# A conditional mix with a mixture of low-rank experts: one engine's bias held back, splits and tails reordered in the first three steps, half of a product moved in the last

## The reference, cut to what matters

```python
x, cond                      # x: (64, 64, 1024) f32, cond: (64,) in 0..15
y = einsum('bct,bcd->bdt', x, W[cond])          # 64 x 64 per batch, 16 conditions
logits = einsum('bsd,ed->bse', y, gate_w)       # 8 experts, the best 2 chosen
gates  = softmax of the best 2, zero elsewhere
low    = einsum('bsd,erd->ebsr', y, lora_A)     # rank 16 for each of 8 experts
result = y @ base_w.T + base_b + 2 * einsum('ebsr,eor,bse->bso', low, lora_B, gates)
out = x + result
```

## Time and profile before

| | |
|---|---|
| time, median of 3 runs | 489.36 us (488.27 to 489.56) |
| time of the profiled execution | 488.3 us |
| its span, first to last instruction | 486.5 us |
| mean granted clock of TensorE | 0.993 |
| busy: PE, DVE, ACT, POOL | 473.6, 353.5, 159.9, 120.7 us |
| moved by DMA | 76.91 MB, mean 158 GB/s |

### The profile page before, as it was taken

How to read it: one execution, slowest core, us unless ns; L and a number is a source line. 1 busy time by engine, 2 the same in 40 slices (tenths; PEclk the granted TensorE clock), 3 DMA queues, 4 the chain that set the end, 5 groups by cost and what they waited for, 6 DMA issues and landing times.

```text
span 486.5 us, 8142 instructions
## 1 busy us (share of the span) xinstructions
PE 473.6 (97%) x2660; PEld 464.0 (95%) x2660; DVE 353.5 (73%) x636; ACT 159.9 (33%) x262; POOL 120.7 (25%) x113
## 2 busy tenths in 40 slices
PE   8995999999999999999999999999999999999996
PEld 8995998989999999999999999999999999999995
DVE  4858679778686785868678685876868677585843
ACT  5723533233332233323323332233324223332300
POOL 2346033132041402304141140413104141310300
PEclk9998999999999999999999999999999999999999
DMA  8972353534626264362536436253552526343202
GB/s 319 412 243 90 148 186 116 177 108 165 204 88 220 63 222 146 141 223 88 187 93 215 152 129 215 84 197 108 190 177 113 208 84 224 109 172 111 88 22 86
DMA packets 49275, 76.91 MB, mean 158 GB/s; under 512 B 13666, under 2 KB 32226, under 8 KB 49250
## 3 DMA queue, kind: packets, MB, share of 16 engines
q1 hardware_dynamic: 37586, 71.88, 42.1%
q10 hardware_dynamic: 11664, 4.72, 3.7%
HBM read 41.98 MB, written 34.60 MB: 157 GB/s over the span
## 4 chain that ended last, share of the span: by engine, by line
PE 89%; DVE 4%; ACT 3%; issue 2%; DMA 2%; ACTq 0%; POOL 0%; DVEq 0%; POOLq 0%
PE acc L886 44%; PE acc L878 27%; PE acc L924 9%; PE mixed L918 8%; DMA low_turns<-scratch 1%; PE acc L1082 1%; DVE y_lo L640 1%; DVE t_lo L604 1%; DVE x_parts L620 1%; ACT r_hi L445 1%; DMA scratch<-low_turns 1%; ACT y_hi L457 0%; DVE t_raw L611 0%; ACT y_whole L478 0%; ACT x_parts L467 0%
## 5 line engine op out<-in xcount | busy, mean ns | idle before, releaser
L382 POOL TENSOR_TENSOR x_sb<-x_sb,bias 128x1024 f32<-128x1024 f32 x32 | 77.3, 2438 | 217.6 <-DVE x_sb L732 198.0
L878 PE MATMUL acc<-r_hi,y_hi 128*128 128x392 f32 x256 | 88.3, 345 | 5.3 <-DVE x_sb L739 5.3
L878 PE MATMUL acc<-r_hi,y_lo 128*128 128x392 f32 x256 | 87.9, 344 | 0.2 <-DVE y_lo L599 0.2
L878 PE MATMUL acc<-r_lo,y_hi 128*128 128x392 f32 x256 | 87.7, 343 | 0.0
L886 PE MATMUL acc<-t_hi,s_hi 128*128 128x384 f32 x224 | 74.9, 334 | 1.0 <-issue 1.0
L886 PE MATMUL acc<-t_lo,s_hi 128*128 128x384 f32 x224 | 74.9, 334 | 0.0
L886 PE MATMUL acc<-t_hi,s_lo 128*128 128x384 f32 x224 | 74.8, 334 | 0.0
L886 PE MATMUL acc<-t_hi,y_hi 128*128 128x384 f32 x216 | 72.3, 335 | 0.0
L886 PE MATMUL acc<-t_lo,y_hi 128*128 128x384 f32 x216 | 72.3, 335 | 0.0
L886 PE MATMUL acc<-t_hi,y_lo 128*128 128x384 f32 x216 | 72.2, 334 | 0.0
L640 DVE TENSOR_TENSOR y_lo<-y_turned,y_hi 128x512 fp32r<-128x512 f32 x60 | 51.4, 896 | 26.9 <-ACT y_hi L513 26.8
(11 more groups left out here) (81 smaller groups left out, 740.7 us busy)
## 6 DMA issues: line engine op xcount, KB each, us to landing
x_sb<-in_x SPq DMA_DIRECT2D x32, 512.0 KB, 4.3
out<-x_sb SPq DMA_DIRECT2D x31, 512.0 KB, 3.1
y_scratch<-y_whole SPq DMA_DIRECT2D x60, 256.0 KB, 2.1
y_moved<-y_scratch SPq DMA_DIRECT2D x120, 128.0 KB, 2.8
t_raw<-in_w_quads SPq DMA_DIRECT2D x4, 768.0 KB, 9.4
scratch<-low_turns ACTq DMA_DIRECT2D x16, 128.0 KB, 1.8
low_turns<-scratch ACTq DMA_DIRECT2D x64, 32.0 KB, 2.3
r_raw<-in_w_plain SPq DMA_DIRECT2D x8, 196.0 KB, 5.2
```

The costliest lines, as they stand in the source:

```text
L382: nc.gpsimd.tensor_tensor(x_sb[:, slot(c), :], x_sb[:, slot(c), :], bias[:, :], ALU.add) \
L878: return nc.tensor.matmul(acc[:, i, 0:NP], y_part[:, i, k, :], w_part[:, k, :], start=(k == 0 and product == 0), stop=(k == KT - 1 and pro ...
```

## The change

- SyncE, step 0: of the two loads of x (c = 4 and 5) the second is issued after the move of pair 1, no longer ahead of it.
- GpSimd, steps 0 and 1: `add_bias` for the next step's pairs waits for `y_ready` 8 (both pairs of y split in step 0) and for `y_ready` 10 (pair 0 of y split in step 1).
- ScalarE, step 0: `lowT_high` goes behind `y_copy(0, 0, 1)` and the two `y_high` of pair 0; the cast of T1 goes behind those of pair 1.
- VectorE, step 0: `y_low` of pair 0 ahead of `lowT_low`; `finish_tails` ahead of the split of x; the first `t_add` last.
- VectorE, step 1: `t_low(2, T3)` comes in here (from step 2), `t_low(4, T4)` goes out (to step 2, behind the splits of the sums, `s_low`); `lowT_low` ahead of the split of x.
- Last step: VectorE does `lowT_low` ahead of the third `take`; TensorE does the first half of P4 (6 matmuls) ahead of its experts, the other 6 at the end as before.
- TensorE's waits on `t_ready` follow the new order of the splits. No instruction that computes or moves data is added or taken away.

```diff
@@ SyncE, step @@
                 if load:
-                    for i in range(2):
+                    for i in range(2 if u > 0 else 1):
...
                 if ahead:
                     move(j, u, 1)
+                if u == 0:
+                    load_x(j, 5)
@@ GpSimd, step @@
                     pool.wait_ge(bias_added, 2)
                     select(0, 0, 2)
+                    pool.wait_ge(y_ready, 8)
...
                     if u > 1:
                         pool.wait_ge(taken, 4 * (s - 2) + 3)
+                    else:
+                        pool.wait_ge(y_ready, 10)
@@ ScalarE, step 0 @@
-            lowT_high(0, 0)
             y_copy(0, 0, 1)
-            x_high(0, 0, 2)
             y_high(0, 0, 0, 0)
             y_high(0, 0, 0, 1)
-            t_high(1, T1)
+            lowT_high(0, 0)
+            x_high(0, 0, 2)
             y_high(0, 0, 1, 0)
             y_high(0, 0, 1, 1)
+            t_high(1, T1)
@@ VectorE, step 0 @@
             turn(0, 0, 0)
-            lowT_low(0, 0)
             y_low(0, 0, 0, 0)
             y_low(0, 0, 0, 1)
+            lowT_low(0, 0)
+            finish_tails(0, 0)
             x_low(0, 0, 2)
-            t_add(1, T1, raw_12, raw_11)
-            finish_tails(0, 0)
...
+            t_add(1, T1, raw_12, raw_11)
@@ VectorE, sums_step (step 1) @@
                 t_add(3, T2, raw_22, t_raw[:, T1, :, :])
+                t_low(2, T3)
                 x_low(j, u, 1)
...
+                lowT_low(j, u)
                 x_low(j, u, 2)
-                t_low(4, T4)
-                lowT_low(j, u)
@@ VectorE, step (2 to 15) @@
+                if u == 2:
+                    t_low(4, T4)
                 if ahead:
                     x_low(j, u, 1)
...
-                if u == 2:
-                    t_low(2, T3)
...
-                take(j, u, 2, 5, 1, 0, 2 * BW)
-                lowT_low(j, u)
+                if ahead:
+                    take(j, u, 2, 5, 1, 0, 2 * BW)
+                    lowT_low(j, u)
+                else:
+                    lowT_low(j, u)
+                    take(j, u, 2, 5, 1, 0, 2 * BW)
@@ TensorE, last_products @@
                 multiply(C22, summed(S3), factor(T3), first=False).then_inc(prod_done, 1)
+                multiply(C21, half(1, 1), factor(T4), ks=range(HALF_K // 2))
                 pe.wait_ge(lowT_ready, s + 1)
                 plain_experts()
...
-                experts(1, C21, 0, BW, fresh=True)
+                experts(1, C21, 0, BW)
...
-                multiply(C21, half(1, 1), factor(T4), first=False).then_inc(lora_done, 1)
+                multiply(C21, half(1, 1), factor(T4), first=False, ks=range(HALF_K // 2, HALF_K)).then_inc(lora_done, 1)
```

More of the change, by code:

```diff
@@ L879, in plain, with multiply @@
                                         start=(k == 0 and product == 0), stop=(k == KT - 1 and product == last))
-            def multiply(bank, left, right, first=True):
+            def multiply(bank, left, right, first=True, ks=range(HALF_K)):
                 left_hi, left_lo = left
                 right_hi, right_lo = right
-                for k in range(HALF_K):
+                for k in ks:
                     for n, (l, r) in enumerate(((left_hi, right_hi), (left_hi, right_lo), (left_lo, right_hi))):
@@ L920, in mix, with experts @@
                     last.then_inc(mix_done, 1)
-            def experts(i, bank, lo, hi, fresh=False):
+            def experts(i, bank, lo, hi):
                 for n, (low_part, lb_part) in enumerate(((lowT_hi, lb_hi), (lowT_hi, lb_lo), (lowT_lo, lb_hi))):
                     last = nc.tensor.matmul(acc[:, bank, 0:hi - lo], low_part[:, i, :], lb_part[:, lo:hi],
-                                            start=(fresh and n == 0), stop=(n == 2), skip_group_check=True)
+                                            start=False, stop=(n == 2), skip_group_check=True)
                 return last
@@ L1029, in step @@
                 if u == 2:
-                    pe.wait_ge(t_ready, 1)
+                    pe.wait_ge(t_ready, 2)
                 multiply(C22, summed(S2), factor(T2), first=False).then_inc(prod_done, 1)
@@ L1035, in step @@
                 if u == 2:
-                    pe.wait_ge(t_ready, 2)
+                    pe.wait_ge(t_ready, 3)
                 multiply(C21, half(1, 1), factor(T4)).then_inc(prod_done, 1)
@@ L1039, in step @@
                 pe.wait_ge(taken, 4 * (s - 2) + 2)
-                if u == 2:
-                    pe.wait_ge(t_ready, 3)
                 multiply(C22, summed(S3), factor(T3), first=False).then_inc(prod_done, 1)
```

## The result

The changed kernel takes **485.97 us** (median of 6, 485.46 to 487.02); the kernel before, timed beside it, 488.56 us. The ratio is 0.9949, with an interval from 0.9937 to 0.9960: faster by 0.5%, or 2.6 us. The forecast was 1.2 us faster, put as 488.1 us: it was taken from the first median of the kernel before, 489.36 us of three executions, and that of all six is 0.8 us lower. The profiled execution has a span of 483.9 us, 2.6 less than before. All executions of the kernel before that were timed beside the experiments have a median of 488.8 us.

A forecast was written before the change was run, and what follows sets the result against it. TensorE, busy for 97% of the span, was taken as the bound, so only its waits, slow clock and program ends could give time; +0.6 - 1.05 - 0.7 = -1.2 us, from 489.36 to 488.1 us; eight in ten from 485.2 to 489.8.

The forecast's parts named there:

- faster rival: Steps 0 and 1: either GpSimd takes fewer turns (486.4 us, chance 0.15) or `t_add` meets no contention (481.7 us, 0.07).
- the slower rival: Step 0: the second move lands late and delays pair 1's turn; over 490.8 us from 2.7 us late on, chance 0.13.
- its second rival: Step 1: no contention with the `t_add`, chain 4.7 us shorter, clock stays up; -7.65 us, 481.7 us, chance 0.07.
- the first case: Stall moves from step 0 to step 1's experts; around 488.1 us, own range 486.9 to 489.4, chance 0.65.
- the rival with fewer turns: Step 1: GpSimd's second addition slips behind the third `t_add`, what follows comes 1.8 us earlier; -3.0, 486.4 us, chance 0.15.
- start of step 2: End of step 1: experts resume 1.3 us earlier but the lower clock costs 1.9 us, so 0.6 us later.
- step 2: With `t_low(2, T3)` out of VectorE's queue, the second `take` precedes TensorE's arrival: -1.05 us; `t_low(4, T4)` stays hidden.
- last step, to the end of the span: Last matmul ends 1.4 us earlier, but the end is a store; -0.7 us taken, between -0.35 and -1.4.
- the two limits: Step 1: `lowT_lo` done at 76.7 us behind GpSimd's second addition, or 75.6 with the DMAs alone setting it.
- the stores' bound (0.35): Last step: the two stores before the last follow the last S1T1 product, which moves by 0.35 us only.
- TensorE's (1.4): Last step: six P4 matmuls fill the stall before the experts but for 0.35 us; last matmul ends 1.4 us earlier.

## Why the prediction was right, and what it mis-sized

**Right.** The stall moved, as forecast, from the tails of step 0 to the experts of step 1, for 6.2 us where 6.6 were said; the clock fell there and not in step 0 (1.00 from 42 to 51 us); the three `t_raw` were stretched to 9.52 us by turns with GpSimd (10.0 were said); step 2 lost its gap, and T4's split that came into it stayed hidden (VectorE still waits 0.80 us for TensorE behind it); the last experts lost their stall. Neither faster rival happened: the turns were two, and the contention was there. The second move of pair 1 was in time: `y_turned` began at 43.11 us, where 43.0 was reckoned, so that the slower rival had nothing to work with. (Of what was said for it, the code loads have DMA queues of their own in the profile, with 0.3 MB in all.)

The Trainium skill's lock ("SBUF — State Buffer", "SBUF: two separate sides") is borne out by more than the change's own rows: beside an addition of GpSimd of about 2.5 us even a VectorE operation of 0.17 us takes 2.38 us. The prediction's sentence that ports shared at some rate would give its second rival does not follow, since that rival had no contention at all; sharing was not priced.

**Mis-sized.** The gain is 2.6 us and not 1.2. 485.97 us lies within the stated range of eight in ten (485.2 to 489.8), but below the first case's own (486.9 to 489.4), and even below the 486.4 us of the rival with fewer turns, whose mechanism did not occur. So the time alone could not have told the cases apart; the profile does. Of the 2.1 us between 488.1 and 485.97, 0.8 are the median that the forecast was applied to. The rest are the terms, and all three erred the same way. By terms of the sum, in the profiles:

| term | forecast | measured |
|---|---|---|
| start of step 2 | +0.6 | -0.21 |
| step 2 | -1.05 | -1.29 (30.03 to 28.74) |
| last step, to the end of the span | -0.7 | -1.1 |
| sum | -1.2 | -2.6 |

*The start of step 2* was the largest error, 0.8 us, in two terms. The first is the step "`lowT_lo` is asked for inside the second addition, waits for its end, and is done at 76.7". The addition ended at 71.22 + 4.64 = 75.86 us and not at 76.3. Half of this is the chain in front of it: a turn cost 2.03 us (9.52 less 5.47 us are 4.05 for two) and not 2.36, a figure for which no row stood, and of what that saved 0.2 us were left when `y_lo` was done, at 71.08 and not 71.3. The other half is the addition itself, 0.14 + 4.64 us behind `y_lo` where 0.2 + 4.8 were reckoned. The way through the DMAs came the other way: from the copy to the cast it was 7.04 us (68.16 to 75.20) and not the 6.47 of step 3, so that `lowT_lo` could start at 75.64 and not at 75.2. So the two limits that the prediction set more than a us apart, with -2.3 us for the DMAs alone, came within a few tenths: here `lowT_lo` took 0.50 us, under 0.1 of it waiting; in the run with T3's split put back, where the DMAs came 0.9 us earlier, it waited about 0.3. It was done at 76.14, 0.6 us before the forecast, and the experts start 1.81 us earlier than before where 1.3 were forecast. The second term is the clock: 4.65 less 3.05 us are 1.6 and not 1.9; the run with TensorE kept busy gives back 1.4 of them. With 1.95 us in the run with T3's split put back, this size is partly chance.

*Step 2:* the stall of 1.05 us has 0.24 us behind it in which the matmuls run below their rate; putting the split back gave 1.3 us.

*The last step:* between the stores' bound (0.35) and TensorE's (1.4) I took 0.7. TensorE's own gain was 1.7 us, more than the bound: besides the stall of 1.4 us, the first nine experts take 1.23 us where they took 1.49 behind it. The stores gave back 0.5. The last store took 2.4 us to land where it took 1.9. That the one ahead delays it, as the prediction said, fits this, but no run tried it; the delay was smaller than laid out.

**What the change's parts are worth**, from the runs: in steps 0 and 1 the two waits alone lose 1.7 us, and the new order turns that into 0.2 us gained. Of its two waits that of step 1 is worth 4.15 us and that of step 0 costs 5.5, each with the other kept. T3's split is worth 1.3 us, the last step 1.2 to 1.5. The stall of step 1 itself was worth more than all of it: with the wait of step 0 out and the ranking early it goes, and the kernel takes 477.0 us.

**Left open:** what decides whether a stall just under 3 us costs the clock (next section); which of the moves within step 0 were needed, since the order of SyncE, ScalarE and VectorE there was only tried as a whole; and which half of the last step's part brought its gain.

## What to carry to other kernels

Where two engines exclude each other from a memory port, do not ask how to keep one out of the other's way but which instructions of the other it will meet instead, and put it on those with room behind them: two additions of GpSimd held VectorE for 0.45 us beside the split of x in step 0, for 4 us beside the differences of weights and for 4 us in the ranking. And look at when the other instruction asks: the same split, asked for just behind the start of the second addition, was held for 2.25 us, and the rest of the chain with it. Room that depends on such a race shows as a spread of the times. When a stall is long enough to move rather than go, follow the chain to the next wait and find its first link; here it was a round trip by DMA. With the additions out of the way of the weights 2.9 us of the stall were left, and they went when the round trip was started earlier. And a wait put in for order's sake should be tried alone as well as with the moves that come with it: of the two here one was worth 4 us and the other cost 5.

## What the runs showed of the hardware that was not expected

- A VectorE operation on 16 columns with two operands from SBUF waits for nearly a whole addition of GpSimd: 2.38 us for 0.17 us. Two in one ranking pay twice.
- The turns are not strictly one for one. Between the two operations of the ranking that waited, `greater`, which has two operands as well, took its usual 0.28 us, though GpSimd's second addition is shown from 64.2 us on. So VectorE got a second short instruction in when its first was served; why isn't shown.
- An instruction of VectorE that asks before GpSimd's first addition has ended goes ahead of the second (the split of x at 39.76 us: 1.67 us). One that asks just behind the second one's start waits for all of it (at 40.25 us, the second shown from 40.2: 3.47 us).
- Stalls of the same length were followed by different clocks. After 2.9 us with the first wait out, the granted clock stayed at 1.00 in the 3 us of experts (2.4 GHz); after 2.8 and 2.9 us with the waits alone it was 0.50 and 0.66 in the 4 us behind. After 6.2 us it was 0.63. The same 18 matmuls took 4.65 us then, 5.00 after 6.1 us of waiting (0.57), 5.11 after 7.2 (0.55) and 5.17 after 10.3 (0.55).
- The executions of one kernel differ in the same way: with the first wait out the mean clock of the whole program was 0.999 to 1.000 in three (480.20 to 480.45 us) and 0.996 in two (481.61 and 481.95).
- A stall leaves a little behind it at the full clock too: 0.25 us over the 36 matmuls behind the gap in step 2, and 4.46 us instead of 4.28 for the 24 matmuls behind the experts in the run without the first wait.
